# A selective-scan pipeline inside a transformer loop: the decay moves to PSUM, the convolution reads its projection in PSUM

## The reference, cut to what matters

```python
proj = h @ in_W + in_b
x1, g = (proj[..., :D], proj[..., D:])                      # D = 256 channels
xc = conv(x1 over tokens, conv_w, padding=[(K - 1, 0)])     # K = 4 taps, each channel by itself
x1 = silu(xc + conv_b)
delta, Bm, Cm = split(x1 @ dbc_W + dbc_b)                   # 16, 16 and 16 columns
delta = softplus(delta @ dup_W + dup_b)
A_disc = exp(delta[..., None] * A)                          # the decay, N = 16 states a channel
B_x = delta[..., None] * Bm[:, :, None, :] * x1[..., None]
hs[t] = A_disc[t] * hs[t-1] + B_x[t]                        # the scan over 256 tokens
y = silu(g) * einsum('tbdn,btn->btd', hs, Cm)
out = y @ out_W + out_b + residual
```

## Time and profile before

| what | value |
|---|---|
| median of 3 runs | 1990.13 us (1988.86 to 1998.07) |
| the profiled execution's own time | 1990.29 us |
| its span | 1988.5 us |
| PE busy | 1774.7 us (89%) |
| DVE busy | 1704.8 us (86%) |
| POOL busy | 1633.2 us (82%) |
| ACT busy | 1262.0 us (63%) |
| mean granted TensorE clock | 0.958 of full |

### The profile page before, as it was taken

How to read it: one execution, slowest core, us unless ns; L and a number is a source line. 1 busy time by engine, 2 the same in 40 slices (tenths; PEclk the granted TensorE clock), 3 DMA queues, 4 the chain that set the end, 5 groups by cost and what they waited for, 6 DMA issues and landing times. The chain is left out here.

```text
span 1988.5 us, 73877 instructions
## 1 busy us (share of the span) xinstructions
PE 1774.7 (89%) x30944; PEld 1004.7 (51%) x30944; DVE 1704.8 (86%) x2592; ACT 1262.0 (63%) x2355; POOL 1633.2 (82%) x1350
## 2 busy tenths in 40 slices
PE   3899999999989999999999999999989899999872
PEld 1455555555545554555555555555545555555520
DVE  5789998989987899889889889888998799998636
ACT  3567757667676576667676675765766676766630
POOL 2778998978988799879898899887998789987851
PEclk9899999999999999999999999999999999999975
DMA  3123432242323423134231523234241443214221
GB/s 101 34 42 56 80 58 53 55 74 38 63 50 78 66 37 61 43 58 83 57 58 31 80 57 58 65 59 63 37 75 34 85 73 54 38 29 74 47 32 42
DMA packets 95606, 113.13 MB, mean 57 GB/s; under 512 B 42334, under 2 KB 61548, under 8 KB 95276
## 3 DMA queue, kind: packets, MB, share of 16 engines
q1 hardware_dynamic: 95276, 108.41, 30.3%
HBM read 19.22 MB, written 1.05 MB: 10 GB/s over the span
## 5 line engine op out<-in xcount | busy, mean ns | idle before, releaser
L1313 POOL TENSOR_TENSOR AB<-qc,qn 128x512 f32<-128x512 f32 x384 | 521.9, 1365 | 25.1 <-DVE qn L1107 24.8
L1324 POOL TENSOR_TENSOR AB<-AB,rinv 128x512 f32<-128x512 f32 x384 | 442.9, 1168 | 43.3 <-DVE rinv L1130 43.3
L544 PE MATMUL bank<-wqkv,XT 128*128 128x512 f32 x768 | 420.6, 631 | 8.4 <-DVE qn L1107 4.9
L824 ACT ACTIVATE sq<-bank 128x512 f32<-128x512 f32 x384 | 227.9, 594 | 160.9 <-PE bank L544 156.4
L1331 POOL TENSOR_TENSOR Pb<-Pb,p_rden 128x512 f32<-128x512 f32 x192 | 211.4, 1101 | 128.7 <-DVE p_rden L1151 127.6
L833 ACT ACTIVATE qkT<-bank 128x512 f32<-128x512 f32 x384 | 229.9, 599 | 100.5 <-PE bank L569 98.1
L1114 DVE TENSOR_REDUCE ssq<-sq 128x8 f32<-128x512 f32 x384 | 255.4, 666 | 37.2 <-ACT sq L824 37.1
L1107 DVE TENSOR_TENSOR qc<-bank,rt 128x512 f32<-128x512 f32 x384 | 258.9, 674 | 32.0 <-ACT sq L824 26.4
L569 PEld LDWEIGHTS bank<-ident,AB 128*128 128x128 f32 x1536 | 175.4, 142 | 196.5 <-issue 103.6
L1107 DVE TENSOR_TENSOR qn<-bank,rt 128x512 f32<-128x512 f32 x384 | 260.6, 679 | 0.0
L618 PEld LDWEIGHTS bank<-PT,V 64*64 64x64 f32 x12288 | 199.7, 136 | 112.8 <-issue 80.5
(11 more groups left out here) (133 smaller groups left out, 2788.1 us busy)
## 6 DMA issues: line engine op xcount, KB each, us to landing
V<-V SPq DMA_DIRECT2D x672, 64.0 KB
rep<-du SPq DMA_DIRECT2D x64, 512.0 KB, 7.5
wqkv<-in_Wqkv SPq DMA_DIRECT2D x36, 256.0 KB, 3.7
XV<-XT SPq DMA_DIRECT2D x96, 64.0 KB, 2.8
wo<-in_Wo SPq DMA_DIRECT2D x6, 512.0 KB
BC<-BC SPq DMA_DIRECT2D x8, 256.0 KB
w<-in_W SPq DMA_DIRECT2D x6, 341.0 KB, 5.7
BC<-BC SPq DMA_DIRECT2D x8, 128.0 KB
```

What stands on the lines that cost most here:

```text
L544: pe.matmul(R[u % 2][:], XT[:, s % NB, (u % 2) * P:(u % 2 + 1) * P], wqkv[:, (u // 2) * 512:(u // 2 + 1) * 512], start=True, stop=True).th ...
L824: act.activation(sq[:, u % 2, :], R[u % 2][:], ACT.Square).then_inc(sq_done, 1)
L1313: pool.tensor_tensor(AB[:, n % NAB, :], qc[:, u % 2, :], qn[:, u % 2, :], ALU.add).then_inc(rs_done, 1)
L1324: pool.tensor_tensor(o, o, r, ALU.mult).then_inc(nm_done, 1)
```

## The change

- **Decay in PSUM.** `z_decay` writes the two halves of bank `M` and `dA` is gone. There is one bank, so a decay waits until the scan before it is done (before, two buffers). `z_scan` is two instructions of 256 elements, one a block, that read the decay from `M`.
- **Convolution from PSUM.** `z_copy_x` and `x1p` are gone. `z_tap` and `z_conv` read the projection in `M`. The bias of the projection is folded into the convolution's: `cvbe = cvb + inb * (sum of the taps)`, and the first three tokens, where fewer taps fall inside, get a small correction `edge`, one more DVE instruction on 128x2x3 elements. `cvbe` and `edge` are computed once in `start_phase`, by eight tiny DVE instructions.
- **Who holds `M`.** `M_ORDER` now has the 16 decays as users too; `z_x` holds the bank until the convolution is done.
- **Buffers.** `NREP` 3 to 4, `NH` 4 to 5.
- **Order and lags.** All five lists are written anew. `z_conv(i)`, the third call of a DVE step before, is now `z_conv(i + 2)`, the last but one. `z_dbc` and `z_dup` come one step later. `FIRST_TO_LAST` starts at -2, so the first convolution stands ahead of the first `rotate` on DVE. The scans of one sequence fall on loop steps so (chunks at lag 3, 4, 5, 6, 7, 8): 1, 4, 2, 4, 2, 3 before and 2, 1, 4, 1, 5, 3 after.

```diff
-NREP = 3
-NA = 2
-NH = 4
+NREP = 4
+NH = 5
...
-M_ORDER = [("z_out", 0, 9, 6), ("z_x", 0, -1, 6), ("z_dbc", 0, 0, 6), ("z_dup", 0, 0, 6), ("z_g", 0, 4, 6)]
+M_ORDER = [("z_x", 0, -1, 6), ("z_dbc", 0, 1, 6), ("z_out", 0, 9, 6), ("z_g", 0, 5, 6), ("z_dup", 0, 1, 6),
+           ("z_decay", 13, 8, 6), ("z_decay", 1, 4, 6), ("z_decay", 6, 6, 6), ("z_decay", 2, 4, 6),
...
+        def m_free(eng, kind, n, s):
+            before = M_BEFORE[kind, n, s]
+            if before is not None:
+                kind, n, s = before
+                b = s // BSTEP
+                sem, count = {"z_x": (conv_done, b + 1), "z_g": (g_copied, 2 * b + 2), "z_dbc": (dbc_copied, b + 1),
+                              "z_dup": (dx_copied, 2 * b + 2), "z_out": (st_done, b + 1),
+                              "z_decay": (scan_done, 16 * b + n + 1)}[kind]
+                eng.wait_ge(sem, count)
...
-                act.wait_ge(x1_copied, 2 * b + 2)
...
-                    ins = act.activation(x1s[:, c, :], x1p[:, c, 0:SEQ], ACT.Identity, scale=cvw[:, c, 0:1],
-                                         bias=cvb[:, c:c + 1])
+                    ins = act.activation(x1s[:, c, :], M[:, c * SEQ:(c + 1) * SEQ], ACT.Identity,
+                                         scale=cvw[:, c, KC - 1:KC], bias=cvbe[:, c:c + 1])
...
-                if n >= NA:
-                    act.wait_ge(scan_done, n - NA + 1)
+                m_free(act, "z_decay", j, s)
...
-                    ins = act.activation(dA[:, n % NA, c, 1:], rep[:, (8 * (s // BSTEP) + r) % NREP, 0, c, 1:], ACT.Exp,
+                    ins = act.activation(M[:, c * SEQ:(c + 1) * SEQ], rep[:, (8 * (s // BSTEP) + r) % NREP, 0, c, :], ACT.Exp,
                                          scale=Aneg[:, col:col + 1])
...
-                        ins = dve.scalar_tensor_tensor(x1s[:, c, :], x1p[:, c, n:n + SEQ], cvw[:, c, n:n + 1],
-                                                       x1s[:, c, :], ALU.mult, ALU.add)
-                ins.then_inc(conv_done, 1)
+                        ins = dve.scalar_tensor_tensor(x1s[:, c, n:], M[:, c * SEQ:(c + 1) * SEQ - n],
+                                                       cvw[:, c, KC - 1 - n:KC - n], x1s[:, c, n:], ALU.mult, ALU.add)
+                    link(ins)
+                dve.tensor_tensor(x1s[:, :, 0:KC - 1], x1s[:, :, 0:KC - 1], edge[:], ALU.add).then_inc(conv_done, 1)
...
-                h = hb[:, n % NH].rearrange("p c t -> p (c t)")
-                dve.tensor_tensor_scan(h, dA[:, n % NA].rearrange("p c t -> p (c t)"), h, 0.0, ALU.mult, ALU.add)\
-                   .then_inc(scan_done, 1)
+                for c in range(DBLK):
+                    h = hb[:, n % NH, c, :]
+                    ins = dve.tensor_tensor_scan(h, M[:, c * SEQ:(c + 1) * SEQ], h, 0.0, ALU.mult, ALU.add)
+                ins.then_inc(scan_done, 1)
```

More of the change, by code:

```diff
@@ L747, in _ @@
             for i in FIRST_TO_LAST:
+                z_x(i + 1)
+                turn_p(i - 1, 3)
+                value(i, 1)
+                value(i, 2)
+                turn(i, 0)
                 values_out(i - 1, 3)
-                turn(i, 0)
-                value(i, 1)
+                value(i, 3)
                 turn(i, 1)
-                value(i, 2)
+                qk(i + 1, 0)
+                qk(i + 1, 1)
+                scores(i, 0)
                 turn(i, 2)
[L754 to L757, removed]
+                z_sum(i - 5, 0)
+                w_out(i - 2, 0)
+                z_dbc(i - 1)
                 turn(i, 3)
-                w_out(i - 2, 0)
-                w_gelu(i - 3, 0)
[L761 to L766, removed]
+                z_out(i - 9)
+                z_g(i - 5)
+                qk(i + 1, 2)
+                z_dup(i - 1)
+                scores(i, 1)
+                qk(i + 1, 3)
+                w_out(i - 2, 1)
+                turn_p(i, 0)
+                w_gelu(i - 3, 0)
+                qk(i + 1, 4)
                 turn(i, 4)
-                z_sum(i - 7, 5)
-                z_out(i - 9)
                 values_out(i, 0)
-                qk(i + 1, 3)
-                w_out(i - 2, 2)
                 w_gelu(i - 3, 1)
                 turn(i, 5)
-                qk(i + 1, 4)
+                qk(i + 1, 5)
+                w_out(i - 2, 2)
                 w_gelu(i - 3, 2)
@@ L1027, in _ @@
-                z_copy_g(i - 5)
-                copy_v(i, 2)
+                square(i + 1, 0)
+                square(i + 1, 1)
                 copy_qk(i, 2)
                 z_decay(i - 4, 2)
+                z_copy_dbc(i - 1)
+                z_decay(i - 6, 7)
+                copy_qk(i, 3)
+                expo(i, 0)
+                z_copy_g(i - 5)
+                z_decay(i - 5, 3)
+                square(i + 1, 2)
+                z_copy_dx(i - 1)
+                z_decay(i - 7, 8)
+                z_exp_x(i)
@@ L1056, in _ @@
                 copy_p(i, 1)
+                z_decay(i - 7, 10)
+                z_decay(i - 5, 4)
                 expo(i, 2)
-                square(i + 1, 5)
+                z_decay(i - 8, 15)
                 copy_qk(i, 6)
+                z_decay(i - 7, 11)
+                z_exp_g(i - 5)
+                square(i + 1, 6)
+                copy_qk(i, 7)
                 copy_o(i, 1)
-                copy_qk(i, 7)
-                z_decay(i - 4, 4)
-                z_decay(i - 3, 0)
-                square(i + 1, 6)
@@ L1272, in _ @@
-                z_scan(i - 5, 6)
-                gate(i - 3, 2)
+                z_scan(i - 4, 2)
+                sum_squares(i + 1, 2)
+                z_scan(i - 7, 9)
+                z_scan(i - 5, 3)
+                sum_p(i, 1)
+                z_state(i - 9)
+                sum_squares(i + 1, 3)
+                rotate(i + 1, 4)
+                rotate(i + 1, 5)
+                softmax(i, 2)
+                sum_squares(i + 1, 4)
+                gate(i - 3, 0)
+                sum_squares(i + 1, 5)
@@ L1274, in _ @@
+                z_scan(i - 7, 10)
+                sum_p(i, 2)
+                z_scan(i - 8, 15)
+                res_attention(i - 2)
+                z_scan(i - 5, 4)
+                gate(i - 3, 1)
+                z_scan(i - 7, 11)
+                rotate(i + 1, 6)
                 sum_squares(i + 1, 6)
                 center(i - 2)
-                sum_p(i, 3)
+                gate(i - 3, 2)
+                softmax(i, 3)
                 sum_squares(i + 1, 7)
                 guard_q(i + 1)
-                rotate(i + 1, 6)
+                sum_p(i, 3)
@@ L1428, in _ @@
-                rotate_sum(i + 1, 1)
+                normalise_p(i, 0)
+                rotate_sum(i + 1, 1)
+                z_hc(i - 4, 0)
+                z_bu(i - 6, 7)
+                z_bu(i - 5, 5)
+                z_bu(i - 7, 11)
+                normalise(i, 6)
+                z_bu(i - 8, 15)
+                rotate_sum(i + 1, 2)
+                rotate_sum(i + 1, 3)
+                normalise_p(i, 1)
+                z_hc(i - 7, 8)
                 z_bu(i - 5, 6)
-                z_hc(i - 8, 12)
@@ new lines, in _ @@
+                normalise(i, 7)
+                rotate_sum(i + 1, 4)
+                rotate_sum(i + 1, 5)
+                z_hc(i - 7, 10)
+                normalise_p(i, 2)
+                z_silu_x(i)
+                z_hc(i - 4, 2)
+                z_silu_g(i - 5)
+                z_hc(i - 8, 15)
+                z_bu(i - 4, 3)
+                z_delta(i - 2)
+                z_bu(i - 4, 4)
+                z_hc(i - 7, 11)
+                z_bu(i - 7, 13)
+                z_bu(i - 3, 0)
+                z_bu(i - 7, 14)
```

293 lines of the change are left out of this document (113 added, 180 removed).

## The result

The changed kernel takes 1929.01 us (median of 4 runs, 1926.95 to 1930.79), against 1989.9 for the kernel before on the same chip: a ratio of 0.9693, interval 0.9661 to 0.9724, or 61 us less. 1920 was predicted, with a range of 1858 to 1990. In what follows a kernel's place is its ratio to the kernel before, run beside it, with a 95% interval; 0.001 is 2 us. Traces are of one execution of each kernel, whose own time can lie some us beside the median.

What follows compares the result with a forecast made beforehand. PE was taken to set half the steps at about 36 us, DVE and POOL together the others. Gains of 34, 9 and 30 us, 73 less 3 for the bank, gave 1990 - 70 = 1920 us, range 1858 to 1990.

Steps and rivals of the forecast that it cites:

- Contention and what carries it: DVE instructions with two SBUF inputs and overlapping POOL instructions lengthen each other; one input in PSUM ends it.
- The term for POOL: Of 121 us of waiting inside POOL's instructions, about 104 us would go, 13 a batch.
- A price of PSUM: 304 DVE instructions newly reading PSUM would pay 5 us by the trace, 20 us by the skill's fixed cycles.
- PE as the floor of a step: A step in which nothing disturbs PE takes about 36 us; PE-bound windows gain nothing.
- The convolution's 34 us "whole": The window with the convolution loses its 4.3 us a batch in full, 34 us over 8 batches.
- The scans' and POOL's 39 us: Relief of scans and POOL: 9 us in the convolution's window, 30 in the windows of 39.45 and 38.87 us.
- 3 more for the bank: Decays waiting for scans in M may halt ACT and then PE: 3 us in all, bounds 0 and 115.
- The new lists: DVE's fullest loop-step load falls from 14 us to 7, the reason to count on both gains.
- The longest step: Sign of being right: the longest step of a batch falls below 39 us.
- The single bank: M has room, about 54 of 230 us a batch; ACT's waits for scans below 10 us, above 50 meaning wrong.
- the rival in which the bank decides: ACT held at the decays loses all the gain: 1980 us with half held, 2038 at worst; chance 0.12.
- Head: "about nothing": The first convolution now holds the first rotation about 4 us, before 7 a few steps later: about nothing.

Runs made afterwards that it cites:

- e6: The changed kernel, decay still in PSUM, with one scan of 512 elements in place of two of 256: 1926.81 us, ratio 0.9689.
- e5: The changed kernel with the decay in one SBUF buffer, scanned by one instruction of 512, two scratch-tile pairs shared: 1989.54 us, ratio 0.999.
- e1: The changed kernel with the decay in one SBUF buffer, still two half scans, two scratch-tile pairs shared: 2020.58 us, ratio 1.0115.
- e8: The changed kernel without the mask's 1536 small matmuls on PE, scores unmasked, for timing only: 1903.28 us, ratio 0.9565.
- e3: The kernel before with only the convolution changed (projection read in PSUM, bias folded in), old lists, buffers and scans: 1980.8 us, ratio 0.9915.
- e11: The changed kernel with only the convolution undone, reading an SBUF copy of its projection: 1944.07 us, ratio 0.9766.
- e9: The changed kernel with one more DVE instruction per chunk, a maximum over 256 elements of M ahead of the scans: 1934.82 us, ratio 0.9696.
- e10: The changed kernel with four small POOL memsets per chunk ahead of each input term: 1986.23 us, ratio 0.9959.

## Why the prediction was right, step by step

**Contention and what carries it: right.** The term for POOL was 104 us and came out as 105 (1633.2 to 1527.8). The means of L1315 and L1326 were to be near 1.29 and 1.06 us and are 1.298 and 1.062. A half scan was taken as 0.70 us and took 0.672, with 0.691 as the longest. The convolution's instructions were taken as 0.475 and took 0.47 to 0.48, its corrections as 0.2 and took 0.27. DVE's busy time was to be near 1620 and is 1596.1: the two halves of a chunk overlap and keep DVE busy for 1.26 us and not 1.40, which is 18 us of it. PE's idle time, which would have spoken against the prediction if it had grown, fell from 213.8 to 171.8 us of the span.

**A price of PSUM: small.** A whole scan of 512 takes 1.212 us on average from PSUM (e6), against 1.199 for the shortest from SBUF and 1.183 in e5: 13 to 29 ns. The shortest are alike, 1.180 from PSUM (e6) and 1.183 from SBUF (e5), and so are those of the halves, 0.648 and, in e1, 0.650. The Trainium skill, VectorE: DVE Perf Modes, section on the TRN2 errata, gives 120 fixed cycles for a PSUM source against 58 for SBUF. The 62 cycles between them would be 65 ns at its 0.96 GHz, as an estimate; the measurement decides, and the small value of the prediction was the better one.

**PE as the floor of a step: right.** Steps without a disturbance were taken as 36 us; in the batch shown they are 34.4 to 36.6 now, and averaged over six batches three are at 34.4 to 36.4 and two still at 37.7 and 38.1. e8 showed that PE's time counts.

**The convolution's 34 us "whole": wrong by a factor of two.** This is the term that was mis-sized. Alone it brought 17 us in the old lists (e3) and 15 in the new (e11). The step said that the window with the convolution has DVE and POOL at 90% and so loses its 4.3 us in full. In e3's trace it did lose 3.4, but neighbouring steps took nearly all of it back, and by the medians about half came through. A window that is 90% full says where time is lost, not that it will stay saved.

**The scans' and POOL's 39 us: too small.** Measured as the placement alone, e5 against e6, 60 us. The prediction treated DVE and POOL as equal partners in it. e9 and e10 say otherwise: DVE had some slack, POOL not. Two parts of the 60 us it did not have: up to 19 lie in the step that waits for V's copies (3.2 us in each of six batches), by that wait or by POOL, and PE is busy for 16 us less in e6 than in e5, with a granted clock of 0.968 against 0.961.

**The sum: close by luck.** From the kernel before to e3, e5 and e6 the steps are 17 us less, 15 more and 60 less, 62 in all. The prediction had 34 less, 3 more for the bank and 39 less, 70 in all. It took 17 us too many for the convolution, 12 too few for the cost between and 21 too few for the scans and POOL. These errors nearly cancelled, which is why 1920 lies 9 us from 1929.

**The new lists: no gain of their own.** The prediction counted on the flatter spread of DVE's work, and DVE's fullest step of a batch did go from 38.6 to 34.0 us. But from e3 (0.9915) to e5 (0.999) the new lists, the buffers and the single decay buffer together cost 15 us while scans collide; the intervals of the two just miss each other. That the scan in PSUM needs the new lists, since its decays take turns in `M`, is argued: no run has it with the old ones. The longest step was to be below 39 us and is 40.6: it is a new one, whose loop step has five scans and seven input terms.

**The single bank: larger waits than said, no visible price.** ACT was to wait below 10 us for scans in all. The waits of ACT and DVE on each other in the changed kernel:

```profile
ACT bank L1015 <- DVE hb L1215: 24.8, 24, 4.8
```

```profile
DVE hb L1215 <- ACT bank L1015: 29.0, 26, 2.2
```

ACT's are 24.8 us, above the 10 said and below the 50 that were named as a sign of being wrong. e9 makes the bank's turn 0.4 us longer for every chunk, ACT's wait rises to 36.3 us, and the time stays. So the rival in which the bank decides is refuted for this order, and with room to spare.

**Head: "about nothing" was 6 us.** The first six steps took 5.4 us more and the start 1.0. The drain, for which there was no term, took 3.4 more.

## What to carry to other kernels

Where DVE and POOL are both busy, look at the spread of a single instruction's time before counting instructions: a line whose median is far above its shortest, beside POOL lines whose longest is far above their median, is two engines stopping each other. Moving one of the two SBUF inputs of the DVE instruction to PSUM frees both; and what that is worth is found by adding dummy work to each engine alone, not by the sum of the busy times. Take from the trace how much of the dummy work arrived, and what the bound engine then waits for. Splitting an instruction that collides can double its collisions (e1 against e5: 25 us).

## What was not expected of the hardware

PE stopped in the middle of groups of small matmuls, waiting for nothing that the profile shows. In the changed kernel:

```profile
PE bank L604 <- issue: 23.9, 14, 3.2
PE bank L633 <- issue: 8.9, 4, 3.6
...
PE bank L584 <- issue: 6.2, 3, 3.2
```

That is 39 us in 21 stops, against 15 us in 9 before, with the same PE instructions. From kernel to kernel they vary between 15 and 46 us, so they blur every difference of a few us here. In the trace's records each stop ends 1.2 to 1.6 us behind the end of one of the 246 packets of the instruction queue (4.03 MB), which fits PE running out of instructions; no run was made to test it. e8, with fewer instructions, has 234 packets and 23 us of stops, but e9 and e10, with 246 packets each, have only 27. Two such stops of 3 us fall into the fifth step, which takes 42.9 us in place of 33.7, and so into the loss at the head.
